# A third buffer for the widened blocks in passes 1 to 3 of a graph network, and what moves with it

## The reference

```python
def _L0_gnn_ref(x, edge_index, W1, b1, gamma, beta, W2, b2):
    agg = jax.ops.segment_sum(x[src], dst, num_segments=x.shape[0])
    h = agg + x
    h1 = h @ W1 + b1                      # 256 -> 1024
    h1 = (h1 - mean) * jax.lax.rsqrt(var + BN_EPS) * gamma + beta
    return jax.nn.relu(jax.nn.relu(h1) @ W2 + b2)
...
def layer(h, W, b):                       # in _L1_gnn_ref, three times
    h = h @ W.T
    msg = h[src] * norm[:, None]
    agg = jax.ops.segment_sum(msg, dst, num_segments=n)
    return jax.nn.relu(agg + b)
...
x = _layernorm(x + _L0_gnn_ref(...), axis=-1)
x = _layernorm(x + _L1_gnn_ref(...), axis=-1)
```

## Time and profile before

| | |
|---|---|
| median of 3 runs | 2821.2 us (2817.2 to 2828.34) |
| span of the profiled execution | 3416.5 us |
| TensorE matmuls busy in it | 2607.3 us, 76% |
| TensorE weight loads | 1908.3 us, 56% |
| VectorE / ScalarE / GpSimd busy | 37% / 31% / 52% |
| DMA, mean | 744 MB, 218 GB/s |
| pass 0 / MLP / passes 1 to 3 in the profile | 1212 / 187 / 2017 us |

### The profile page before, as it was taken

One profiled execution on the slowest core, in us unless ns is written; L12 is line 12 of the kernel. 1 busy time (PEld: TensorE's weight loads), 2 busy tenths in 40 slices (PEclk: granted clock), 3 DMA queues, 4 the chain that ended last, 5 costly groups with the idle time before them and its releaser, 6 DMA issues.

```text
span 3416.5 us, 43495 instructions
## 1 busy us (share of the span) xinstructions
PE 2607.3 (76%) x15428; PEld 1908.3 (56%) x15428; DVE 1258.9 (37%) x3358; ACT 1074.6 (31%) x1676; POOL 1779.5 (52%) x1896
## 2 busy tenths in 40 slices
PE   2456777777777789679898876788988768888875
PEld 2234455554555577557676644565766546666654
DVE  6665555544445556302121221031313311314133
ACT  0012223322222155334343322333333223333330
POOL 5455555445455300356666664665666556565663
PEclk6568888888878899889999987999999878999997
DMA  4646666656555379668787875676869756767783
GB/s 135 227 161 215 187 202 205 201 193 195 193 172 177 126 250 331 228 190 264 252 261 237 281 232 166 205 258 225 271 222 299 228 184 221 243 220 246 228 284 96
DMA packets 405708, 744.04 MB, mean 218 GB/s; under 512 B 44567, under 2 KB 211543, under 8 KB 399587
## 3 DMA queue, kind: packets, MB, share of 16 engines
q0 software_dynamic: 91056, 263.84, 24.9%
q1 hardware_dynamic: 159731, 245.54, 21.4%
q10 hardware_dynamic: 154688, 231.65, 20.6%
HBM read 610.06 MB, written 130.77 MB: 217 GB/s over the span
## 4 chain that ended last, share of the span: by engine, by line
PE 49%; another core or an unknown queue 15%; issue 13%; DVE 9%; DMA 7%; ACT 5%; DVEq 1%; ACTq 1%; SPq 0%; POOL 0%; POOLq 0%
PE ps L1295 22%; PE ps L1130 7%; PE ps L1188 5%; PE ps L1161 5%; PE ps L1116 3%; PE ps L1198 3%; DMA xs<-in_x_dram 3%; ACT wide L973 2%; DMA hbuf<-parts_d 2%; PE ps L1150 2%; ACT strips L834 2%; DMA us<-in_x_dram 1%; DVE vreg L1495 1%; DVE lnst L1597 1%
## 5 line engine op out<-in xcount | busy, mean ns | idle before, releaser
L788 POOL DMA_INDIRECT ring<-table_d,idx x1236 | 1181.2, 956 | 817.8 <-issue 335.8
L1295 PE MATMUL ps<-wide,hbuf 128*128 128x512 f32 x4116 | 1109.6, 423 | 150.6 <-ACT wide L973 79.2
L1295 PEld LDWEIGHTS ps<-wide,hbuf 128*128 128x128 f32 x4116 | 805.0, 203 | 400.3 <-issue 142.9
L788 POOL DMA_INDIRECT ring<-in_x_dram,idx x592 | 583.0, 985 | 581.6 <-PE ps L1097 378.5
L973 ACT CAST wide<-abuf 128x1024 fp32r<-128x1024 uint8 (+1 forms) x588 | 551.5, 941 | 848.6 <-PE ps L1295 415.3
L1130 PE MATMUL ps<-place,strips 128*128 128x128 f32 x1828 | 311.6, 323 | 244.4 <-ACT strips L834 150.4
L1441 DVE TENSOR_TENSOR acc<-acc,ps 128x256 f32 x230 | 95.5, 415 | 968.8 <-PE ps L1130 545.4
L1130 PEld LDWEIGHTS ps<-place,strips 128*128 128x128 f32 x1828 | 273.4, 226 | 317.8 <-ACT strips L834 194.5
L1161 PE MATMUL ps<-wide,hbuf 128*128 128x512 f32 x784 | 275.1, 481 | 26.8 <-DMA hbuf<-parts_d 13.7
L1116 PE MATMUL ps<-ring,hot 128*32 128x256 f32 x3656 | 269.6, 414 | 26.2 <-DVE place L1455 12.0
L834 ACT COPY strips<-ps 128x512 f32<-128x512 f32 x230 | 133.5, 580 | 451.8 <-remote 283.5
(11 more groups left out here) (144 smaller groups left out, 1791.5 us busy)
## 6 DMA issues: line engine op xcount, KB each, us to landing
hbuf<-parts_d ACTq DMA_DIRECT2D x84, 1024.0 KB
abuf<-ad_d ACTq DMA_DIRECT2D x63, 1024.0 KB
hbuf<-parts_d ACTq DMA_DIRECT2D x84, 768.0 KB
hbuf<-parts_d SPq DMA_DIRECT2D x196, 256.0 KB
parts_d<-vreg SPq DMA_DIRECT2D x72, 512.0 KB, 6.3
h_d<-ureg SPq DMA_DIRECT2D x23, 1024.0 KB
ureg<-h_d POOLq DMA_DIRECT2D x23, 1024.0 KB, 8.1
ad_d<-vreg SPq DMA_DIRECT2D x28, 800.0 KB
```

What stands on the lines that cost most here:

```text
L788: pool.indirect_dma_start(out=ring[:, i % slots, j, :], out_offset=None, in_=table[0:N, :], in_offset=at).then_inc(g["rows"][i % slots], 16)
L1295: ins = pe.matmul(ps[:, 2 + 4 * q + h, 0:(n1 - 4 * q) * P].rearrange("p (s n) -> p s n", n=P), hbuf[:, bl, e * D + h * P:e * D + (h + 1) * P],
```

## The change

`wide` gets a third buffer, `wide2`, which lies behind the second `abuf` in what was padding. `widened(k)` picks the buffer k % 3. The number of buffers, `WIDES` = 3, takes the place of the 2 in the wait of `widen` and in `feed`, so that `feed(k)` widens block k+3. Block 2 is widened ahead of pass 1, behind the MLP's last activation. `load_block`, `load_rows` and the order of the two calls in `feed` are as they were.

```diff
+WIDES = 3
...
         abuf.append(sb("abuf1", [P, MSG, 2 * PAIRS * P], U8))
-        sb("between", [P, KCOLS + HT * CHUNK - (2 * ACOLS + BCOLS + 2 * MSG * P)])
+        wide2 = sb("wide2", [P, MSG, P], F32R)
+        sb("between", [P, KCOLS + HT * CHUNK - (2 * ACOLS + BCOLS + 3 * MSG * P)])
+
+        def widened(k):
+            return wide[:, k % WIDES, :, :] if k % WIDES < 2 else wide2[:, :, :]
...
                 if bl == 0:
                     act.wait_ge(s_ld[n % 2], (n // 2 + 1) * 16)
-                wait(act, s_step, k - 1)
+                wait(act, s_step, k - WIDES + 1)
                 ns = NSG[k // NB % ND]
-                act.copy(wide[:, k % 2, 0:ns, :], one_block(abuf[n % 2][:, 0:ns, :], n % DLOADS, bl)).then_inc(s_wide, 1)
+                act.copy(widened(k)[:, 0:ns, :], one_block(abuf[n % 2][:, 0:ns, :], n % DLOADS, bl)).then_inc(s_wide, 1)
                 if bl == BLOCKS - 1 and n + 2 < 3 * ND * DLOADS:
                     load_block(n + 2)
 
             def feed(k, stored_by):
 
                 n, bl = k // BLOCKS, k % BLOCKS
-                if k + 2 < 3 * STEP:
-                    widen(k + 2)
+                if k + WIDES < 3 * STEP:
+                    widen(k + WIDES)
                 if bl in (FRONT - 1, BLOCKS - 1) and n + 1 < 3 * ND * DLOADS:
                     load_rows(n + 1, bl // FRONT, stored_by)
...
             act.wait_ge(mlps["relu"], NCH1 * HT)
+            widen(2)
             load_block(1)
...
-                                            wide[:, k % 2, 4 * q:n1, :],
+                                            widened(k)[:, 4 * q:n1, :],
```

## The result

The changed kernel takes 3077.4 us (median of 4 runs, 3070.1 to 3086.9), the kernel before 2819.2 us beside it: ratio 1.093, 95% interval 1.090 to 1.097. That is 258 us slower, where 106 us were forecast, and outside the range, which ended at 3040 us.

What follows compares the result with a forecast made beforehand. TensorE bounds passes 1 to 3, busy 1617 of 2017 us. Terms -30 (third buffer), +132 and +34 (late hbuf loads), -8 sum to +128 us, scaled to 106: 2925 us, range 2815 to 3040 us.

Steps and rivals of the forecast that it cites:

- The mechanism: ScalarE's DMA queue: abuf's load moves ahead of hbuf's first load, which lands 10.9 to 13.7 us after the widening.
- the budget of three steps: Time from issuing the next hbuf's first load to step 0 needing it: 7.2, 9.0, 10.8, 11.1 us, mean 9.5.
- The load term: Passes 1 to 3, hbuf's first load late: +132 us full-length blocks, +34 us half-length, -8 us for hbuf's last rows.
- The low bound: hbuf's first load landing 10.9 us after the widening, said to be beyond two of the four budgets.
- The third buffer's gain: TensorE's waits before dense steps: one more step in hand during ScalarE's pauses, taken as -30 us.
- the rival: Faster: third buffer takes up ScalarE's pauses at the 35 waits before dense steps, some 40 us, giving 2780 us; chance 0.14.
- The scaling by 0.826: Whole sum: loads and budgets both shrink from the profiled span to the median, so 128 us becomes 106 us.
- The rival "much slower": DMA engines bound: without the profiler budgets shrink 17% and loads don't, +210 us, 3031 us; chance 0.18.
- the waits for strips: TensorE's waits for ScalarE's copy of the strips in passes 1 to 3: to stay near 150 us.
- those for the widened block: TensorE's waits for the widened block: to fall from 79.2 us, by less than half.
- the `hbuf` waits, to be 1 to 4 us each: TensorE at step 0 of most blocks: hbuf waits to grow from 16.6 us to over 100 us.
- the forecast's +3.7%: Whole kernel: forecast slowdown, to 2925 us.

Runs made afterwards that it cites:

- rows_first: Changed kernel with load_rows called before widen in feed, so the first hbuf load is queued ahead of the abuf load: 2808.5 us, ratio 0.998 to before.
- block_back: Changed kernel (third buffer, lead of three steps) with load_block issued in feed of step 4 again, as before the change: 2814.0 us, ratio 1.001.
- two_rows_late: Kernel before, two buffers, with the first hbuf load issued in step 4 behind the abuf load instead of step 3: 3317.0 us, ratio 1.175.
- half_3: Changed kernel leaving out half of the bytes of all but the earliest abuf loads, compared without pauses: 2874.3 us, ratio 1.021 to before.
- rows_first_again: Third buffer with the first hbuf load queued ahead of the abuf load, compared where ScalarE pauses: ratio 0.991 to before.

## Why the prediction was wrong

**The mechanism** was right for the two loads. The wait of the widening is the same, ScalarE is no earlier; A went ahead of R0; R0 landed 11.95 us after the widening (forecast 10.9 to 13.7); the budget of three steps doesn't hold it; 69 of the 73 waits stand at step 0. `rows_first`, `block_back` and `two_rows_late` show that the order of these two loads is the cause.

**The size** was wrong, 106 us for 258. The two profiles without pauses give the account: spans 3070.4 - 2810.2 = 260 us, of which `hbuf` waits are 242.2 - 40.1 = +202 us, busy time of the dense matmuls 1108.5 - 1040.1 = +68 us, strips 33.0 - 41.5 = -8 us. Against the terms of the sum:

- *The load term*, 132 + 34 - 8 = 158 us, or 131 us after the scaling, measured 202. By the count of steps its three parts are +168 us at step 0 of the 63 full-length runs (0.6 us before, 168.3 us in 53 waits after) for 132, +47 us at step 0 of the half-length ones for 34, and -13 us for R1 at step 4 for 8. The step that failed most is the budget of the full-length runs. I took 9.5 us from a profile with pauses, which stretch the three steps that R0 has. All 63 budgets have a median of 9.2 us there and of 7.6 us without pauses. With the latter, the prediction's own sum at 10.9 us gives a shortfall of 2.8 us a run where it took 2.1; the waits are 168.3 / 63 = 2.7 us. That they meet so well is partly luck, as the sum leaves out the later landing and the layers in between. The low bound was also misread by a little: 10.9 us is beyond three of the four budgets, not two; the sum had the third one's 0.1 us.
- *The third buffer's gain*, -30 us, measured 0. The pauses aren't the program's. Where they are, the term is 30 to 50 us, so its size was fair for a condition in which the median had not been taken. The sign of this was in the text: ScalarE stood still for nothing in the program, and the median was 595 us less. I used it to weaken the rival and still booked the 30 us.
- *The clock*: no term at all, measured +68 us, the largest thing left out. The dense matmuls are busy longer though they are the same 4116. The mean granted clock of passes 1 to 3 is 0.97 in the kernel before without pauses and 0.92 in the changed one (columns as in the earlier trace rows):

```profile
1178.00:2810.00 1632.00, 1481.99 (x8666) 1126.76 (x8664) 466.69 (x1117) 680.94 (x861) 1184.55 (x1236) 0.97 0.86 283
...
1190.00:3070.00 1880.00, 1558.64 (x8650) 1181.61 (x8650) 464.69 (x1117) 675.55 (x857) 1176.82 (x1231) 0.92 0.74 244
```

The changed kernel's stretches around the wait of 2.72 us show where it comes from:

```profile
1301.20:1306.60 5.40, 5.40 (x26) 4.45 (x25) 1.11 (x2) 2.34 (x3) 4.15 (x5) 1.00 0.43 113
1315.30:1318.50 3.20, 3.20 (x8) 2.52 (x9) 0.00 (x0) 0.00 (x0) 2.59 (x3) 0.50 1.01 383
1318.50:1322.40 3.90, 3.90 (x18) 2.98 (x16) 0.00 (x0) 2.10 (x2) 1.01 (x2) 1.00 0.54 198
1337.30:1344.60 7.30, 7.30 (x32) 6.02 (x33) 0.00 (x0) 3.15 (x3) 5.47 (x7) 1.00 0.64 209
```

Ahead of the wait the granted clock is 1.00, that is 2.4 GHz; for 3.2 us behind it 0.50, 1.2 GHz, with 8 matmuls where the earlier trace rows has 24 in 5.72 us, or 13 in 3.2 us; then 1.00 again. So this wait cost about 1.5 us more than its own length (24 matmuls took 7.23 us against 5.72 us in the earlier trace rows). After the wait of 1.91 us the clock stayed at 1.00. But the length of a wait doesn't decide it alone. Two more waits of the same run, 1.97 us and 2.91 us, with the clock behind each:

```profile
1379.93 5.50 PE L1301 MATMUL ps<-wide,hbuf 128*128 128x512 f32 x16 [1.97 <-DMA hbuf<-parts_d]
...
1380.00:1383.40 3.40, 3.40 (x8) 2.75 (x9) 0.00 (x0) 0.00 (x0) 2.60 (x3) 0.50 1.05 403
...
1446.42 5.73 PE L1301 MATMUL ps<-wide,hbuf 128*128 128x512 f32 x24 [2.91 <-DMA hbuf<-parts_d]
...
1446.50:1450.00 3.50, 3.50 (x16) 2.89 (x17) 0.00 (x0) 1.05 (x1) 2.58 (x4) 1.00 0.88 310
```

The shorter one was followed by half the clock and the longer one was not; what decides between them isn't shown here. Over whole runs, longer waits go with longer dense matmuls. In `half_3` the waits are 108.4 us in 55, mean 2.0 us, against 3.3 us, and its dense matmuls are at 1052.4 us, only 12 over before. In `two_rows_late` they are 441.0 us in 84, mean 5.3 us, and the dense matmuls are 119 us over before.

- *The scaling by 0.826* went the wrong way. It turned 128 into 106 us, as if loads shrank with the span. They didn't: 11.95 us from the widening is inside the range taken from the profile with pauses, and only the budgets shrank. The rival "much slower", at 3031 us, had said just this and was the nearest. Its nearness is partly luck: it has 50 us without a row, books the third buffer's 30 us too, and has no clock either.

Together, of the 154 us between 106 and 260: the load term, scaled, is 71 us too small, the clock is 68 us, the third buffer's scaled gain 25 us, and the strips go 8 us the other way; that makes 156 us.

Two signs that the prediction named missed with the pauses: the waits for strips were to stay near 150 us and were 33.0, and those for the widened block were to fall by less than half and are gone. And the `hbuf` waits, to be 1 to 4 us each, go up to 10.0 us.

Where there are pauses the forecast's +3.7% stands against +1.3% measured. There the terms were too large: `hbuf` waits rose by 102 us over `rows_first_again` (121.3 - 19.2) and not by 158. The time rose by 76 us (3472.8 - 3396.6) and not by 102; TensorE's waits for strips are lower in the changed kernel, 136.4 us against 201.8, so its new waits in part replace others. That this is the whole of it wasn't tried.

## What to carry to other kernels

A lead is not a private matter of one buffer: whatever else hangs on the same index (here a load at the end of a run) moves with it, past what stands in the same queue. For each load ask how many steps lie between where it can be issued and where it is needed, and compare this time with the landing time of all that is ahead of it in the queue. A profile whose span is far from the runs' median shows another condition of the machine; read mechanisms from it, but don't book its idle time as something to win, don't scale its terms, and take budgets from the steps' busy times (three steps of 1.9 us are 5.7 us here, and the shortest budget in either profile was 5.4 us).

The version to keep is the third buffer with R0 ahead of A, or with the split load: 0.998 (0.995 to 1.002) and 0.998 (0.996 to 1.001) without pauses, 0.991 (0.989 to 0.994) and 0.987 to 0.989 with them. The split on two buffers is the only one whose interval lies below 1 without pauses, 0.997 (0.995 to 0.999), and that by very little.

## What the runs showed of the hardware

The same program took 2809 to 2819 us in some comparisons and 3381 to 3430 us in others, 20% apart, with no median of this kernel in between. In the second kind ScalarE, and TensorE behind it, stand for nothing that the profile shows, up to 15 us at a time, as in the earlier trace rows; the granted clock is lower too (0.87 against 0.93). The cause wasn't tried.

Waits of 2 to 3 us can cost TensorE's clock: one of 2.72 us and one of 1.97 us were followed by more than 3 us at 1.2 GHz, one of 1.91 us and one of 2.91 us were not. In the changed kernel the slower clock made a quarter of the loss.

Loads in ScalarE's queue waited for what was ahead of them: 1 MB behind 1 MB landed 10.23 us after its issue, where 1 MB with nothing ahead of it had moved its bytes in 5.1 us. Swapping the two issues gave all 258 us back (2808.5 us).
